# Layers on all context rows, rows gathered by indirect DMA, FFN weights in a ring: one Trainium2 core

## The reference

```
def gat_layer(x, adj, W, a_self, a_neigh, b):
    feat = einsum('nf,hfo->hno', x, W)
    e = leaky_relu(self[:, :, None] + neigh[:, None, :]) + MASK_VAL * (1.0 - adj)   # MASK_VAL = -1e10
    out = einsum('hnm,hmo->hno', softmax(e), feat) + b
    return elu(out)                                        # heads side by side: [512, 512]
x = x + gat_layer(gat_layer(ctx, layernorm(x), W0, ...), layernorm(x), W1, ...)
x = x + ffn(layernorm(x))      # row n goes to expert n % 4: silu(x@gate) * (x@up) @ down, inner width 512
```

## Time and profile before

| | |
|---|---|
| time, median of 3 runs (lowest, highest) | 267.31 us (266.08, 267.94) |
| span of the profiled execution | 265.9 us |
| profiled execution's own time | not given apart from its span |
| PE busy | 228.9 us, 1046 matmuls |
| DVE, POOL, ACT busy | 177.7, 131.8, 111.1 us |
| granted PE clock, mean | 0.957 |
| moved by DMA | 23.83 MB |

### The profile page before, as it was taken

How to read it: one execution, slowest core, us unless ns; L and a number is a source line. 1 busy time by engine, 2 the same in 40 slices (tenths; PEclk the granted TensorE clock), 3 DMA queues, 4 the chain that set the end, 5 groups by cost and what they waited for, 6 DMA issues and landing times.

```text
span 265.9 us, 2980 instructions
## 1 busy us (share of the span) xinstructions
PE 228.9 (86%) x1046; PEld 184.0 (69%) x1047; DVE 177.7 (67%) x285; ACT 111.1 (42%) x156; POOL 131.8 (50%) x98
## 2 busy tenths in 40 slices
PE   0598997999559999999509999999999997989990
PEld 0387875887347888888307888887878876868870
DVE  3899598999996999170029999272089986940041
ACT  1447987634335821270165840283076025320100
POOL 1305493676960376100991177159529887850100
PEclk9999999999958999999956999999999999999998
DMA  5999254000260000040373000057700220400004
GB/s 178 378 334 218 80 168 148 4 0 0 79 226 14 0 0 1 2 158 0 97 234 143 4 0 0 0 161 230 229 15 4 77 79 0 159 2 0 0 7 157
DMA packets 14754, 23.83 MB, mean 90 GB/s; under 512 B 6672, under 2 KB 6672, under 8 KB 14736
## 3 DMA queue, kind: packets, MB, share of 16 engines
q1 hardware_dynamic: 12432, 19.41, 23.3%
q10 hardware_dynamic: 2304, 4.20, 4.8%
HBM read 19.41 MB, written 4.19 MB: 89 GB/s over the span
## 4 chain that ended last, share of the span: by engine, by line
PE 59%; DVE 24%; issue 7%; POOL 4%; DMA 3%; ACT 1%; SPq 1%; DVEq 0%; POOLq 0%; ACTq 0%
PE bank L1385 29%; PE bank L1403 14%; PE bank L1350 10%; DVE ctx_xn L1116 4%; DVE top L999 3%; DMA x_sb<-in_x 3%; DVE exps L1070 2%; DVE val L1096 2%; PE bank L1328 2%; DVE G L1004 2%; DVE exps L1073 2%; DVE xstat L1033 2%; PE bank L1367 2%; POOL x_sb L755 2%; PE bank L1288 1%
## 5 line engine op out<-in xcount | busy, mean ns | idle before, releaser
L1385 PE MATMUL bank<-xnT,GUp 128*128 128x512 f32 x288 | 72.3, 409 | 9.2 <-issue 9.2
L1385 PEld LDWEIGHTS bank<-xnT,GUp 128*128 128x128 f32 x288 | 56.7, 197 | 23.6 <-issue 9.6
L1403 PE MATMUL bank<-DNp,parts 128*128 128x512 f32 x192 | 47.1, 394 | 2.0 <-issue 1.0
L1350 PE MATMUL bank<-W1p,parts 128*128 128x512 f32 x192 | 45.9, 396 | 1.4 <-issue 1.0
L780 POOL TENSOR_TENSOR parts<-sil,parts 128x512 fp32r<-128x512 f32 x15 | 20.2, 1348 | 48.2 <-ACT parts L937 48.2
L1350 PEld LDWEIGHTS bank<-W1p,parts 128*128 128x128 f32 x192 | 35.8, 188 | 10.8 <-issue 1.4
L1403 PEld LDWEIGHTS bank<-DNp,parts 128*128 128x128 f32 x192 | 35.6, 188 | 10.6 <-issue 1.9
L740 POOL TENSOR_TENSOR GUp<-stage,GUp 128x1024 fp32r<-128x1024 f32 x12 | 28.7, 2417 | 12.3 <-issue 8.3
L1130 DVE TENSOR_TENSOR sil<-bank,sil 128x512 f32<-128x512 f32 x16 | 10.9, 684 | 32.8 <-PE bank L1385 31.2
L937 ACT CAST parts<-sil 128x512 fp32r<-128x512 f32 x16 | 10.0, 622 | 50.4 <-DVE sil L1130 50.4
L755 POOL TENSOR_TENSOR x_sb<-x_sb,val 128x512 f32<-128x512 f32 x16 | 21.6, 1352 | 14.9 <-DVE val L1096 14.9
(11 more groups left out here) (88 smaller groups left out, 333.2 us busy)
## 6 DMA issues: line engine op xcount, KB each, us to landing
stage<-in_L_ffn_gate_up_proj SPq DMA_DIRECT2D x16, 512.0 KB, 3.3
stage<-in_L_ffn_down_proj SPq DMA_DIRECT2D x8, 512.0 KB, 3.5
out<-x_sb ACTq DMA_DIRECT2D x16, 256.0 KB, 2.7
x_sb<-in_x SPq DMA_DIRECT2D x6, 512.0 KB, 8.3
stage<-in_L_xattn_W SPq DMA_DIRECT2D x5, 256.0 KB, 7.3
x_sb<-in_x SPq DMA_DIRECT2D x4, 256.0 KB, 4.3
ctx_xn<-in_ctx SPq DMA_DIRECT2D x4, 256.0 KB, 8.0
b_rows<-in_L_xattn_b SPq DMA_DIRECT2D x1, 256.0 KB
```

The source lines that it names most:

```text
L1350: last = nc.tensor.matmul(y_bank(e, b)[:, :], parts[:, h_slot(e, c), w, b * P:(b + 1) * P], W1p[:, c, v, :], start=(c == 0 and j == 0), st ...
L1385: last = nc.tensor.matmul(bank[4 + 2 * (c % 2) + half][:, :], gu_parts(e, k)[:, w, col:col + P], xnT[:, k, v, :], start=(k == 0 and j == 0 ...
L1403: last = nc.tensor.matmul(bank[b][:, :], parts[:, in_slot(n), w, b * P:(b + 1) * P], DNp[:, i, v, :], start=(i == 0 and j == 0), stop=(i = ...
```

## The change

The layers no longer wait for the selection. They run over all 512 context rows of each graph in their own order: `turn_ctx` transposes the loaded context, `layer0(b)` and `layer1(b)` run graph by graph, and y goes by SP to a table in DRAM, y_table[b]. PSUM banks of y are seeded with b1 by ACT (`seed`), three in turn, and DVE's elu reads them there. The selection is now of indices: DVE's MAX8 and MAX_INDEX give f(n) (`find`); SP stores it to f_table; POOL's indirect DMAs read f(f(n)) from it (`follow`, 128 rows of 4 bytes each, 16 of them) and then row f(f(n)) of y_table, added by the DMA to the x tile (`gather`, 128 rows of 2 KB, 16). The one-hot matmuls, `sel_ctx`, `residual` and y's bias add are gone. The FFN starts after all layers; its weights go through `ring`, eight chunks of 128x1024 in high and low part, in the order in which PE uses them, and gate and up are loaded by column block c, both in one fill. Maxima for the bound are taken over rows, in the FFN stage, from data loaded again.

The core of the diff; lists of names, sizes, and helpers that only take a new index are left out.

```diff
-EXPS = 5
+RING = 8
+HEXP = 3
+YB = 3
...
+    y_table = [nc.dram_tensor(f"y_table{b}", [N, D], F32).ap() for b in range(B)]
+    f_table = [nc.dram_tensor(f"f_table{b}", [N, 1], U32).ap() for b in range(B)]
...
+        KINDS = (("G", 0), ("G", 1), ("D", 0), ("G", 2), ("G", 3), ("D", 1))
...
+            def store_y(n):
+                sp.wait_ge(y_made, n + 1)
+                sp.dma_start(y_rows[n // E][n % E], val[:, n % E, :]).then_inc(y_stored[n % E], 16)
...
+            def follow(b, e, signal):
+                if e == 0:
+                    pool.wait_ge(f_stored[b], 16)
+                nc.gpsimd.indirect_dma_start(
+                    out=ff_row[:, b, e:e + 1], out_offset=None, in_=f_table[b][:, :],
+                    in_offset=bass.IndirectOffsetOnAxis(ap=f_row[:, b, e:e + 1], axis=0)).then_inc(signal, 16)
+            def gather(b, e):
+                if e == 0:
+                    for t in range(E):
+                        pool.wait_ge(y_stored[t], 16 * (b + 1))
+                    pool.wait_ge(ff_first[b], 16)
+                else:
+                    pool.wait_ge(ff_rest[b], 16 * (E - 1))
+                pool.wait_ge(xstat_made, B * e + b + 1)
+                nc.gpsimd.indirect_dma_start(
+                    out=x_sb[:, b, e, :], out_offset=None, in_=y_table[b][:, :],
+                    in_offset=bass.IndirectOffsetOnAxis(ap=ff_row[:, b, e:e + 1], axis=0),
+                    compute_op=ALU.add).then_inc(gathered[b][e], 16)
...
+            gather(2, 0)
+            gather(3, 0)
+            x2_inverse_std(0, 0)
+            x2_inverse_std(0, 1)
+            for b in range(B):
+                for e in range(1, E):
+                    follow(b, e, ff_rest[b])
+            for b in range(B):
+                gather(b, 1)
+            w_low(FIRST + 5)
             for e in range(E):
...
+            def seed(n):
+                if n < YB:
+                    act.wait_ge(warm_done, n + 1)
+                else:
+                    act.wait_ge(y_made, n - YB + 1)
+                nc.scalar.copy(bank[n % YB][:, :], b1_rows[:, :]).then_inc(y_seeded, 1)
...
+            w_high(0)
+            ctx_high(1)
+            w_high(1)
+            w_high(2)
+            act.wait_ge(b1_loaded, 16)
+            for n in range(YB):
+                seed(n)
...
+                    y_exp_of(n)
+                    if 0 < b < B - 1:
+                        if t > 0:
+                            h_high(b + 1, t - 1)
+                            h_exp_of(b + 1, t)
+                    if n + YB < B * E:
+                        seed(n + YB)
+                    if t == E - 1:
+                        if 0 < b < B - 1:
+                            h_high(b + 1, t)
+                        if b < 2:
+                            ctx_high(b + 2)
...
+            def y_value(n):
+                dve.wait_ge(y_exp, n + 1)
+                nc.vector.tensor_scalar(yexp[:, n % YB, :], yexp[:, n % YB, :], 1.0, -1.0, ALU.min, ALU.add)\
+                    .then_inc(y_neg, 1)
+                dve.wait_ge(y_neg, n + 1)
...
+                nc.vector.tensor_tensor(val[:, n % E, :], bank[n % YB][:, :], yexp[:, n % YB, :], ALU.max)\
+                    .then_inc(y_made, 1)
+            def find(b, e):
...
+                nc.vector.max(top8[:, b, e, :], x_sb[:, b, e, :]).then_inc(top_found, 1)
+                dve.wait_ge(top_found, E * b + e + 1)
+                nc.vector.max_index(found[:, b, e, :], top8[:, b, e, :], x_sb[:, b, e, :]).then_inc(row_found, 1)
...
+            turn_ctx(0)
+            turn_ctx(1)
+            layer0(0)
+            layer0(1)
+            layer1(0)
+            turn_ctx(2)
+            layer0(2)
+            layer1(1)
+            turn_ctx(3)
+            layer0(3)
+            layer1(2)
+            layer1(3)
             for b in range(B):
+                turn_xn(0, b)
```

More of the change, by code:

```diff
@@ L429, in build @@
         flag = sb("flag", [1, 1], I32)
-        ctx_sb = ctx_xn[:, :, :].rearrange("p b (e f) -> p b e f", e=E)
         xn = ctx_xn
[L433 to L474, removed]
+        hT = acts
+        xnT = acts
+        W1p = wide
+        inner_parts = wide
+        sil = hexp
         main.close()
@@ L722, in _ @@
+            sp.dma_start(yexp[:, 0, :].rearrange("p (h o) -> p h o", h=H), W0.rearrange("h f o -> f h o"))\
+              .then_inc(again_loaded, 16)
+            for f in range(FIRST + 14, FILLS):
                 load_fill(f)
@@ new lines, in _ @@
+            for f in range(FIRST):
+                w_low(f)
+            for c in range(KC):
+                h_low(1, c)
+            w_low(FIRST)
+            w_low(FIRST + 1)
+            follow(0, 0, ff_first[0])
+            for c in range(KC):
+                h_low(2, c)
+            w_low(FIRST + 2)
+            follow(1, 0, ff_first[1])
+            for c in range(KC):
+                h_low(3, c)
+            follow(2, 0, ff_first[2])
+            gather(0, 0)
+            w_low(FIRST + 3)
@@ new lines, in _ @@
+                if e == 0:
+                    ctx_maximum()
+                if e == 1:
+                    small_maxima()
+                if e == E - 2:
+                    for t in range(B * E):
+                        nc.vector.bn_aggr(xmv[:, t, :], xstat[:, t // E, t % E, :]).then_inc(xmv_made, 1)
+                if e == E - 1:
+                    check_rows()
+                inner(e, 2)
+                inner(e, 3)
+                inner_low(e, 3)
+                if e + 1 < E:
+                    for b in range(B):
+                        turned_low(e + 1, b)
@@ new lines, in turn_xn @@
+            def turn_xn(e, b):
+                pe.wait_ge(xn_made, B * e + b + 1)
+                if e == 0:
+                    pe.wait_ge(h_made, KC * B)
+                else:
+                    pe.wait_ge(in_made, KC * (e - 1) + 3 + b // 2)
+                for k in range(KC):
+                    last = nc.tensor.transpose(bank[4 + b][:, k * P:(k + 1) * P], xn[:, b, k * P:(k + 1) * P],
+                                               ident[:, :])
+                last.then_inc(xn_turned, 1)
```

1013 lines of the change are left out of this document (423 added, 590 removed).

## The result

The changed kernel takes 304.31 us (median of 4 runs, 302.84 to 304.68); the kernel before, on the same chip, 266.69 (265.26 to 267.94). The ratio is 1.141, 95% interval 1.137 to 1.145: slower by 14%. The forecast was 277, range 257 to 289. The sign was right, the size was not. The profiled execution has a span of 301.8 us, where the forecast's own sum was 275.4.

The account below looks back on a forecast made before the run. It took the kernel as bound by stage: PE on selection, DVE in two experts' layers, then PE. FFN start at 117.8, work, clock and POOL stalls to 269.1, tail 6.3: 275.4; plus 1.4 to the median, 277, range 257 to 289.

Parts of the forecast that it names:

- the unit cost of an indirect DMA: POOL's issue of each follow or gather: 0.75 us, between SP's plain 0.34 and its many-piece 1.14.
- 12 follows (9.0) ... 4 gathers (3.0): POOL's issues before the first down projection, 9.0 and 3.0 us, part of a list ending at 137.6.
- the 6.2 of idle time at the first down projection: PE, ready at 131.4 us, waits 6.2 for POOL and loses another 2.4 of clock.
- 2.4 for the clock at the start: At the start of the FFN, PE's lowered clock adds 2.4 us to the 138.9 of work.
- POOL has ... 24 us of work in 34.7 us of PE, and the ring is filled ahead: After the first down projection's wait, POOL's 24 us of splits, inner_low, roots and gathers fit in 34.7 of PE.
- The chain into the FFN: From last y at 106.2 through store, gather, statistics and transposes to gate and up at 117.8 us, all bare.
- the queue is empty by then: Why a gather's landing was taken as 3.5 us, near a store's 2.7 rather than a crowded load's 7.3.
- The layers: PE and DVE take turns until 106.2 us; PE idles 8 us before layer 0 of graphs 2 and 3.
- the arithmetic of the FFN: FFN matmuls and transposes at full pace take 138.9 us of PE, with 2.4 more for the clock.
- the earlier trace's 9.2 us: PE's idle time before expert 1 in the kernel before, put down to filling the single weight buffer.
- GpSimd's DMAs are heavy: Rival: POOL's issues cost 1.14 us each, giving 283, or 289 with pairs of 1.52; chance 0.14.
- The change doesn't do what it says: Rival: indices or their check fail and the general program runs, over 500 us in all; chance 0.01.

Follow-up runs that it names:

- follows_early: Changed kernel with the follows of experts 1 to 3 issued behind the first follow of their graph; 293.31 us, ratio 1.102.
- write_gather: Changed kernel with the 16 gathers writing their rows instead of adding them to x, so the residual is left out; 294.04 us, ratio 1.109.
- gathers_late: Changed kernel with the gathers of experts 2 and 3 on POOL behind inner_low(e, 2) instead of before inner_low(e, 1); 294.28 us, ratio 1.106.
- loads_held: Changed kernel with SP holding all loads behind FFN fill 5 until graph 3's first gather has landed; 300.53 us, ratio 1.127.
- ctx_early: Changed kernel with the context of graphs 2 and 3 turned, cast and split during graphs 0 and 1; 295.43 us, ratio 1.113.
- combo3: Changed kernel with follows, finds and contexts 2 and 3 earlier, context reload and gathers of experts 2 and 3 later, loads held; 269.62 us, ratio 1.015.

## Why the prediction was wrong

**Where the 26.4 us lie** (301.8 measured, 275.4 in the forecast's sum). Layers: last y at 110.5 instead of 106.2, 4.3. From there to gate and up: 19.7 instead of 11.6, 8.1. FFN: 165.1 (130.2 to 295.3) instead of 151.3, 13.8. Tail: 0.2.

**The step that failed** is the unit cost of an indirect DMA, and every sum with it: "I take 0.75 between them ... and keep both ends", 0.34 and 1.14. It measured 1.25 for a follow and some 1.88 for a gather, both above the upper end. "12 follows (9.0) ... 4 gathers (3.0)" were 15.0 and 7.5, and the 6.2 of idle time at the first down projection was 15.5. follows_early (11.0) and write_gather (10.3) show it. Of the FFN's 13.8 us, this stall is 9.3; the two later waits of PE and their clock, the next point, are 9.0; and terms that were too long, such as 2.4 for the clock at the start, take some back. The nearest rows had not been near: SP's issues took 0.34 and 1.14 us, and the adding, 0.6 on POOL, was in neither. An operation that no row shows needed a wider bound.

**The second fault is one of method.** "POOL has ... 24 us of work in 34.7 us of PE, and the ring is filled ahead" is a sum over an expert. PE however waits at each `inner_low`, and between the first and the second PE gives POOL one gate and up and one down projection, 8.2 us. In that slot stood two roots, four gathers (7.5) and a split, 12 us. The measured waits of 2.0 and 4.6 us and 2.3 of clock are this; gathers_late took 10.0 away by moving eight instructions. Even at 0.75 a gather the slot would have held 2.0 + 3.0 + 2.4 + 1.35 = 8.75.

**The chain into the FFN** was said to be bare, rightly, but had 11.6 where 19.7 were due. The changed kernel's chain of waits has its parts:

```profile
109.78 0.69 DVE val L1005
...
111.14 4.36 DMA ff_row<-f_table,f_row
115.65 0.68 issue
116.33 7.37 DMA x_sb<-y_table,ff_row
123.72 0.70 DVE x2stat L1026
```

The last store was not what the gather waited for: it was graph 3's follow (f ready at 108.4, the follow issued at 111.1 and landed at 115.5), which the forecast left out. And the landing was 3.5 in it, 7.4 in the trace. The loads beside it are 2.2 of that (5.14 in loads_held). The adding is 1.7 by write_gather's median, but this very gather took 7.50 there without it, so the two do not simply add up. That "the queue is empty by then" was wrong; DMA was busy for 0.70 of that window, and the loads cost the follow and the gather some 4 us together. The Trainium skill's law (DMA: Bandwidth & Descriptors, Anatomy of one DMA) gave an estimate of 2.6 for it; the shortest landing here is 4.8 us, 3.3 without the adding, so the measurement decides against it.

**The layers** went as told: two engines in turn, two waits before layer 0 of graphs 2 and 3 (5.2 and 8.1 us, where the forecast had 8 twice), the lower clock behind them. The last y came 4.3 us late. The DVE groups answer to the pair of the earlier trace rows and to the earlier trace rows:

```profile
L1000 DVE TENSOR_SCALAR yexp<-yexp 128x512 f32<-128x512 f32 x16 | 13.4, 834 | 18.8 <-ACT yexp L868 18.8
L989 DVE SCALAR_TENSOR_TENSOR hexp<-bank,b_col,hexp 128x512 f32<-128x512 f32 x16 | 12.0, 751 | 0.6
L1005 DVE TENSOR_TENSOR val<-bank,yexp 128x512 f32<-128x512 f32 x16 | 11.1, 692 | 0.5
L1014 DVE FIND_INDEX8 found<-top,x_sb 128x8 uint32<-128x512 f32 x16 | 10.9, 684 | 0.0
```

A pair of y is 1.53, one of h 1.31 (L986 has a mean of 0.56), where I took 1.3. The mean of y hides two kinds: 13 of the 16 L1000 took 0.41 to 0.43 us, and three took 2.12 to 3.34, each beside a split of weights on POOL. Two of the three stood at the end of the layers, on the path:

```profile
98.53 3.34 DVE L1000 TENSOR_SCALAR yexp<-yexp 128x512 f32<-128x512 f32 x1 [2.38 <-ACT yexp L868]
```

```profile
98.60 2.98 POOL L717 TENSOR_TENSOR ring<-stage,ring 128x1024 fp32r<-128x1024 f32 x1
```

They are 4.6 us longer than usual together, which is about what the layers were late; no run tests it. A find is 0.68 for MAX8, 0.09 and 0.68 for the index: 1.46 instead of 1.3. ctx_early took both waits away and gained 8.9 us.

**Right:** the arithmetic of the FFN within 2% (combo3), the tail (6.5 for 6.3), and that the reduction over partitions would be nearly hidden in expert 2. **The wrong reason for the stall before:** I took the earlier trace rows's 9.2 us for the single buffer's, and they were POOL's 14.4 us of idle time around the reduction, which stood in my own. The forecast of the change did not rest on it, but the better kernel did.

**The rivals.** "GpSimd's DMAs are heavy" named the right mechanism, with 0.14 and too low a ceiling: 1.14 per issue. Its other half, pairs of 1.52, was true for y alone. For descriptors, which it left open, the traces now have rows: four TENSOR_SCALAR of DVE (L1040) took 2.21 us together from 157.86 on, 0.55 each as usual, though a gather's issue ran beside them for 0.9 us, and that issue took 1.63, where the others take 1.53 to 1.60. So the issue's own length made it dear, not DVE. "The change doesn't do what it says" had 0.01: two of the 53 executions of the changed kernel and its variants took about 550 us, and their cause is open.

## What to carry to other kernels

Price an indirect DMA on the engine that issues it, per instruction of 128 rows, and put it where nobody waits for that engine; its landing is several us, and loads beside it lengthen the last one. Check an in-order engine slot by slot between the instructions that others wait for, not by its sum over a stage. And before building a new plan to remove a wait, look at which engine sat idle on "issue" in front of it: here one reduction moved in the old kernel (257.7 us) gave more than the new plan with all its repairs (269.6).

## What the runs showed of the hardware

- An indirect DMA on POOL: 0.94 us busy and 0.30 to the next, for 128 rows of 4 bytes as for 128 rows of 2 KB; 1.55 and 0.30 with the adding. Median landings 3.8 us plain and 5.5 with the adding, for 256 KB; one on the path took 7.4 beside loads and 5.1 without them.
- POOL's split of 128x1024 blocked a DVE instruction with two SBUF inputs for as long as two of them ran back to back (5.56 us for 0.69). A TENSOR_SCALAR with one SBUF input took 3.34 for 0.42 beside one split. POOL's issues of gathers held up neither kind: they overlapped L1073 for 0.3 us and four L1040 for 0.9.
- PE's clock was at 1.00 from 130 to 136 us in the changed kernel although PE had been idle for 17.4 us until 125.1; 16 transposes (3.7 us, at 0.50 from 126 to 128) lay between. So the forecast's 2.4 us for the clock there did not fall due, and the 48 matmuls behind them took 11.2 us. In combo3, with 14.6 us idle and the same 16 transposes, they took 13.1, and the clock was at 0.50 until 124 us. No run shows what decides between the two.
